# Reordering an expert loop: where a weights' copy, the first rows' turn and the optional pairs stand

## The reference

```python
# x: [2048, 256], E = 8 experts, top 2 of each token; w1, w3: [8, 256, 1024], w2: [8, 1024, 256]
logits = x @ gate_w
mult, sel = _sparse_mixer_routing(logits)
w = jnp.sum(mult[:, :, None] * (sel[:, :, None] == jnp.arange(E)[None, None, :]), axis=1)
h = jax.nn.silu(jnp.einsum('th,ehf->etf', x, w1)) * jnp.einsum('th,ehf->etf', x, w3)
out = jnp.einsum('etf,efh,te->th', h, w2, w)
x = _layernorm(x + out)
```

## Time and profile before

| | us |
|---|---|
| median of 3 executions (700.98 to 705.46) | 701.7 |
| the profiled execution, its time | 703.86 |
| its span, first to last instruction | 701.9 |
| PE busy | 593.3 (85% of the span) |
| DVE busy | 452.1 (64%) |
| POOL busy | 282.4 (40%) |
| ACT busy | 245.5 (35%) |
| mean granted PE clock | 0.913 |

### The profile page before, as it was taken

How to read it: one execution, slowest core, us unless ns; L and a number is a source line. 1 busy time by engine, 2 the same in 40 slices (tenths; PEclk the granted TensorE clock), 3 DMA queues, 4 the chain that set the end, 5 groups by cost and what they waited for, 6 DMA issues and landing times.

```text
span 701.9 us, 14082 instructions
## 1 busy us (share of the span) xinstructions
PE 593.3 (85%) x3500; PEld 462.3 (66%) x3501; DVE 452.1 (64%) x1284; ACT 245.5 (35%) x471; POOL 282.4 (40%) x199
## 2 busy tenths in 40 slices
PE   6999899797798885376997989989899898999740
PEld 2444469485475664365876878878788787888640
DVE  2566688765748869865556747667577575767524
ACT  3555530012767542222223232332422324222204
POOL 7000020012444456574715666166661665721112
PEclk9999999899799786567998999999999999999965
DMA  8999409004000043221583948649496385455326
GB/s 271 326 335 336 126 1 241 0 1 180 2 1 1 31 174 128 99 99 47 125 229 68 257 73 218 148 82 256 70 260 117 61 233 126 90 97 92 52 32 223
DMA packets 80214, 93.17 MB, mean 133 GB/s; under 512 B 20912, under 2 KB 76080, under 8 KB 78128
## 3 DMA queue, kind: packets, MB, share of 16 engines
q1 hardware_dynamic: 63088, 78.80, 38.6%
q0 software_dynamic: 6864, 9.11, 7.4%
q10 hardware_dynamic: 10224, 4.79, 4.4%
HBM read 42.67 MB, written 31.67 MB: 106 GB/s over the span
## 4 chain that ended last, share of the span: by engine, by line
PE 60%; DVE 15%; issue 8%; ACT 5%; DMA 5%; ACTq 4%; POOL 2%; SPq 0%; DVEq 0%; POOLq 0%
PE bank L2288 23%; PE bank L2310 11%; PE bank L1869 7%; PE bank L2028 4%; DVE region L1334 2%; DVE region L1332 1%; ACTq L1133 1%; DMA xcol<-xcol 1%; PE bank L1919 1%; PE bank L1878 1%; DMA total<-region,rid 1%; PE bank L2177 1%; DVE small L1351 1%; PE bank L1885 1%; PE bank L2300 1%
## 5 line engine op out<-in xcount | busy, mean ns | idle before, releaser
L2288 PE MATMUL bank<-experts_w,experts_x 128*128 (+1 forms) x864 | 222.2, 408 | 18.6 <-DVE experts_x L1713 18.5
L2288 PEld LDWEIGHTS bank<-experts_w,experts_x 128*128 128x128 f32 x864 | 162.1, 194 | 54.5 <-issue 19.0
L888 POOL DMA_INDIRECT total<-region,rid x36 | 55.7, 1548 | 145.3 <-DVE region L1803 91.4
L2310 PEld LDWEIGHTS bank<-experts_w 128*128 128x128 f32 x840 | 107.2, 195 | 7.4 <-issue 4.5
L1779 DVE TENSOR_TENSOR xcol<-region,bank 128x512 f32<-128x512 f32 x72 | 49.4, 686 | 97.2 <-ACT region L1148 96.3
L2310 PE MATMUL bank<-experts_w 128*128 x840 | 108.6, 286 | 4.0 <-issue 4.0
L1148 ACT ACTIVATE region<-bank 128x512 f32<-128x512 f32 x72 | 42.2, 597 | 142.5 <-PE bank L2288 60.3
L761 POOL TENSOR_TENSOR small<-small 128x4 f32<-128x4 f32 (+5 forms) x19 | 25.0, 1318 | 108.0 <-DVE small L1343 87.5
L1154 ACT CAST experts_w<-bank 128x512 fp32r<-128x512 f32 x70 | 40.6, 586 | 68.2 <-DVE bank L1788 61.7
L1869 PE MATMUL bank<-xcol,region 128*128 128x512 f32 x128 | 57.9, 610 | 7.6 <-DMA xcol<-in_xT 6.0
L868 POOL TENSOR_TENSOR experts_w<-wstage,experts_w 128x4096 f32 x6 | 53.9, 8988 | 24.9 <-ACT experts_w L1163 24.9
(11 more groups left out here) (355 smaller groups left out, 897.3 us busy)
## 6 DMA issues: line engine op xcount, KB each, us to landing
xcol<-xcol SPq DMA_DIRECT2D x140, 128.0 KB
slots<-padrow SPq DMA_DIRECT2D x8, 2210.0 KB, 19.4
wstage<-in_w_exp SPq DMA_DIRECT2D x6, 2048.0 KB, 9.1
wstage<-in_w_exp SPq DMA_DIRECT2D x2, 3072.0 KB, 11.8
wstage<-in_w_exp SPq DMA_DIRECT2D x6, 1024.0 KB, 5.6
region<-slots ACTq DMA_DIRECT2D x36, 128.0 KB
xcol<-in_xT SPq DMA_DIRECT2D x4, 512.0 KB, 7.2
xtok<-in_x SPq DMA_DIRECT2D x1, 2048.0 KB, 13.6
```

The costliest lines, as they stand in the source:

```text
L888: pool.indirect_dma_start(out=total, out_offset=bass.IndirectOffsetOnAxis(ap=rid[:, s:s + 1], axis=0), in_=yout[:, s], in_offset=None, com ...
L2288: mm = pe.matmul(bank[2 * u + m][:, :], (xTh, xTl)[a][:, s, k, :], moving(off, w, m * KD * F + k * F + u * HALF, HALF), start=(k == 0 and ...
L2310: mm = pe.matmul(bank[6][:, 0:D], (high, low)[a][:, u, c, :], moving(off, w, 2 * KD * F + (4 * u + c) * D, D), start=(u == 0 and c == 0 an ...
```

## The change

- **ACT:** a block opens with `silu(g, 0)`; then the row load, `silu(g, 1)`, `high_turned(g-1)`, and `high_up(g)` at the end.
- **Rows:** one transfer of 260 columns into `xg` takes the place of the two; it waits for both the turned rows and the metadata of the block whose buffer it takes. DVE works out `row_meta(g+1)` in block g and keeps the result in `kept` (`keep_meta`). `rows(g+1)` stands ahead of `middle(g, 0)`.
- **Weights:** 2048 + 2048 + 2048 columns are loaded in blocks g+1, g+2, g+3 behind an event block g, each after its own part is used up; `tab_load` becomes a mask of three bits. POOL's order is `send_block(g-2)`, `split_down(g-1)`, `low_up(g)`, the last in two halves.
- **Start:** PE turns block 0's rows ahead of the early down; `row_meta(0)` moves ahead of the loop.
- **Loops:** `all_pairs` runs the optional pairs first and the 14 required ones behind them, with the number of optional ones in a register `more`.

```diff
+        def all_pairs(eng, pair):
+            more = eng.value_load(tab_n[0:1, 3:4], min_val=0, max_val=NB // 2 - SURE)
+            with eng.Fori(0, NB // 2 - SURE) as it:
+                with eng.If(more - it > 0):
+                    pair(it + 2)
+            with eng.Fori(0, SURE - 2) as it:
+                pair(it + (more + 2))
...
             def load_ahead(g):
-                with sp.If(sp.value_load(tab_load[0:1, bass.ds(g - 1, 1)], min_val=0, max_val=1) > 0):
-                    event = event_of(g - 1)
-                    e = expert_of(event + 2)
-                    sp.wait_ge(w_low_up, event)
-                    load_up(e)
...
+                begun = sp.value_load(tab_load[0:1, bass.ds(g, 1)], min_val=0, max_val=7)
+                far = not isinstance(g, int) or g > 3
+                with sp.If(begun > 0):
+                    for n in range(2 if far else 1):
+                        with sp.If((begun & (1 << n)) > 0):
+                            event = event_of(g - (n + 1))
+                            e = expert_of(event + 2)
+                            sp.wait_ge(w_low_up, 2 * event + n)
+                            load_up(e, n)
+                    if far:
+                        with sp.If((begun & 4) > 0):
+                            event = event_of(g - 3)
+                            e = expert_of(event + 2)
+                            sp.wait_ge(w_ready, event + 2)
+                            load_down(e)
...
-                pool.tensor_tensor(lo_of(off)[:, 0:ACT_PART], wstage[:, 0:ACT_PART], hi_of(off).bitcast(F32)[:, 0:ACT_PART],
-                                   ALU.subtract).then_inc(w_low_up, 1)
+                for half in range(2):
+                    part = slice(half * UP_PART, (half + 1) * UP_PART)
+                    pool.tensor_tensor(lo_of(off)[:, part], wstage[:, part], hi_of(off).bitcast(F32)[:, part],
+                                       ALU.subtract).then_inc(w_low_up, 1)
...
+                    if not isinstance(g, int) or g >= 2:
+                        send_block(g - 2, s)
+                        with pool.If(begins(g - 1)):
+                            split_down(g - 1)
                     with pool.If(begins(g)):
                         low_up(g)
...
             def load_rows(g, s):
-                rows = slots[bass.ds(slot_of(g), P), :]
+                slot = slot_of(g)
                 act.wait_ge(xg_turned, g - 1)
-                act.dma_start(xq[:, s], rows[:, 0:D]).then_inc(xq_loaded[s], 16)
...
+                act.sem_inc(act_gate, 1)
+                act.wait_ge(meta_done, g - 1)
+                act.dma_start(xg[:, s], slots[bass.ds(slot, P), :]).then_inc(xg_loaded[s], 16)
...
                 for s in range(2):
                     g = 2 * p + s
-                    start = isinstance(g, int) and g < 2
-                    if start and g == 0:
-                        silu(g, 0)
+                    silu(g, 0)
+                    if isinstance(g, int) and g == 0:
                         silu(g, 1)
...
                     load_rows(g + 2, s)
-                    load_meta(g, s)
-                    if not start:
-                        high_up(g)
-                    silu(g, 0)
                     silu(g, 1)
                     for u in range(2):
                         high_turned(g - 1, u)
-                    if start:
-                        high_up(g)
+                    high_up(g)
...
-            dve.tensor_copy(tab_load[:, :], evblk[:, :])
+            link(dve.memset(cmps[:, 0:NB + 3, 0], 0.0))
+            for n in range(3):
+                link(dve.scalar_tensor_tensor(cmps[:, n + 1:n + 1 + NB, 0], evblk[:, :], float(1 << n), cmps[:, n + 1:n + 1 + NB, 0],
+                                              ALU.mult, ALU.add))
+            dve.tensor_copy(tab_load[:, :], cmps[:, 0:NB + 3, 0])
...
-                    row_meta(g - 1, 1 - s)
+                    rows(g + 1, 1 - s)
                     middle(g, s, 0)
-                    rows(g + 1, 1 - s)
+                    keep_meta(g - 1, 1 - s)
+                    row_meta(g + 1, 1 - s)
                     middle(g, s, 1)
...
                     mm = pe.transpose(o[:, c * P:(c + 1) * P], fmid[:, u, c * P:(c + 1) * P], ident[:, :])
                 fill(("fhT", u), mm)
+            turn_rows(0, 0)
             o = claim("fy")
...
                     if isinstance(g, int) and g == 0:
-                        turn_rows(g, s)
                         up(g, s, 0, slot_at[0])
...
-            with pe.Fori(0, SURE - 2) as it:
-                pair(it + 2)
-            with pe.Fori(0, NB // 2 - SURE) as it:
-                with pe.If(npair - it > SURE):
-                    pair(it + SURE)
+            all_pairs(pe, pair)
```

More of the change, by code:

```diff
@@ L450, in decoder_kernel @@
         w_up_loaded, w_down_loaded, w_low_up = (sem(n) for n in ("w_up_loaded", "w_down_loaded", "w_low_up"))
-        xq_loaded = [sem(f"xq{s}_loaded") for s in range(2)]
-        xm_loaded = [sem(f"xm{s}_loaded") for s in range(2)]
+        xg_loaded = [sem(f"xg{s}_loaded") for s in range(2)]
+        meta_kept = sem("meta_kept")
         grouped = [sem(f"h{s}_grouped") for s in range(2)]
@@ L598, in _ @@
                 sp.wait_ge(w_ready, 2)
-                load_up(expert_of(2))
+                e = expert_of(2)
+                for half in range(2):
+                    load_up(e, half)
             regroup(2, 0)
@@ L609, in pair @@
                 load_ahead(2 * p)
-            with sp.Fori(0, SURE - 2) as it:
-                pair(it + 2)
-            with sp.Fori(0, NB // 2 - SURE) as it:
-                with sp.If(npair - it > SURE):
-                    pair(it + SURE)
+            all_pairs(sp, pair)
             for s in range(2):
-                for landed, count in ((xq_loaded[s], 16 * npair + 16), (xm_loaded[s], 16 * npair), (y_sent[s], 16 * npair + 16 * s)):
+                for landed, count in ((xg_loaded[s], 16 * npair + 16), (y_sent[s], 16 * npair + 16 * s)):
                     sp.wait_ge(landed, count)
@@ L867, in low_up @@
                 pool.sem_inc(pool_gate, 1)
-                pool.tensor_tensor(lo_of(off)[:, 0:ACT_PART], wstage[:, 0:ACT_PART], hi_of(off).bitcast(F32)[:, 0:ACT_PART],
-                                   ALU.subtract).then_inc(w_low_up, 1)
+                for half in range(2):
+                    part = slice(half * UP_PART, (half + 1) * UP_PART)
+                    pool.tensor_tensor(lo_of(off)[:, part], wstage[:, part], hi_of(off).bitcast(F32)[:, part],
+                                       ALU.subtract).then_inc(w_low_up, 1)
             def split_down(g):
                 event, off = event_of(g), next_off(g)
-                pool.wait_ge(w_low_up, event)
+                pool.wait_ge(w_low_up, 2 * event + 1)
                 pool.wait_ge(w_down_loaded, 16 * event)
@@ L1775, in _, with keep_meta @@
             first_weigh()
+            row_meta(0, 0)
+            def keep_meta(g, s):
+                dve.wait_ge(meta_done, g + 1)
+                if not isinstance(g, int) or g >= 2:
+                    dve.wait_ge(yout_done, g - 1)
+                dve.tensor_copy(kept[:, s], meta[:, s, 3:5]).then_inc(meta_kept, 1)
             def middle(g, s, u):
@@ L2246, in first_up, with turn_rows @@
                     fill((name, u), mm)
+            def turn_rows(g, s):
+                pe.wait_ge(xg_loaded[s], 8 * (g - s) + 16)
+                if isinstance(g, int) and g == 0:
+                    wait_drained(pe, ("f3", 1))
+                else:
+                    pe.wait_ge(xgT_done, g)
+                for k in range(KD):
+                    mm = pe.transpose(bank[7][:, k * P:(k + 1) * P], xg[:, s, k * P:(k + 1) * P], ident[:, :])
+                mm.then_inc(xg_turned, 1)
             turn_norm2(B - 2)
@@ L2291, in up @@
                 mm.then_inc(up_done, 1)
-            def turn_rows(g, s):
-                pe.wait_ge(xq_loaded[s], 8 * (g - s) + 16)
-                if isinstance(g, int) and g == 0:
-                    wait_drained(pe, ("f3", 1))
-                else:
-                    pe.wait_ge(xgT_done, g)
-                for k in range(KD):
-                    mm = pe.transpose(bank[7][:, k * P:(k + 1) * P], xq[:, s, k * P:(k + 1) * P], ident[:, :])
-                mm.then_inc(xg_turned, 1)
             def down(g, u, off, high, low):
```

96 lines of the change are left out of this document (32 added, 64 removed).

## The result

Over 20 executions of each kernel the changed one takes 701.8 us in the median and the one before 704.6; the ratio is 0.9957, with a 95% interval of 0.9938 to 0.9976. That is faster by 0.4%, about 3 us, and within 1%. The forecast was 3.9% faster (674.6, range 669 to 686): it was wrong.

What follows compares the result with a forecast made beforehand. PE alone was taken to bound ordinary blocks (8.68 us), with stalls where experts begin. Terms -24.3 + 1.6 - 4.5 - 4.5 + 4.6 = -27.1 us took the profiled 703.86 to 676.8, or 674.6 against the median; range 669 to 686.

Steps and rivals of the forecast that it cites:

- Silus open, copy ends: six events: ACT at the six blocks beginning an expert: copying weights after the Silus removes PE's stalls and slow matmuls, -24.3 us.
- ready weights late behind four-block experts: POOL's chain of low parts readies weights 0.8 us late after four-block experts; two of three pay, +1.6 us.
- start of the expert stage: Turning first rows ahead of the early down brings tables and block 1's rows sooner: -4.5 us (bounds 0 and -6).
- skip in the middle: Skipping six optional pairs between blocks 7 and 8 idles PE 3.3 us, plus 1.3 slow matmuls: +4.6 us.
- skip gone from the end: Without skipped pairs behind the loop, DVE's last product starts 4.0 us sooner, final matmuls run faster: -4.5 us.
- The slack of 1.0 us: Block after a weights' copy: the late Silu's product frees PE's bank at G+16.3; PE wants it at G+17.4.
- The lead: PE's sequencer reaches the loop's end 2.3 us before the last matmul ends, so only that much skipping hides.
- Rival 1: The optional-pair skip hides in PE's instruction queue, so the +4.6 vanishes: 670.0 us, chance 0.10.
- the late Silu (2): Silu behind the weights' copy comes late anyway, stalling each expert 1 to 2 us: 684 to 688, chance 0.09.
- the ready weights (3): Ready weights bound short experts; three stall 2 to 3 us, +6 to +9: 681 to 684, chance 0.10.
- the ordinary period is 8.68 us (5): Slower: extra registers for block numbers eat PE's sequencer lead, lengthening 28 blocks; 1.5 us each gives 717, chance 0.03.
- The early turn (4): Turning first rows early brings nothing, because landing scatters, not tables, hold block 1's row load: 679 us, chance 0.06.

Runs made afterwards that it cites:

- K: The changed kernel with the metadata kept by two one-column tensor_scalar instructions instead of one two-column tensor_copy, same place and waits: 682.3 us, 0.9658 of before.

## Why the prediction was wrong, step by step

| step | forecast, us | K's profile, us |
|---|---|---|
| Silus open, copy ends: six events | -24.3 | -24.4 |
| ready weights late behind four-block experts | +1.6 | +1.2 |
| start of the expert stage | -4.5 | -2.4 |
| skip in the middle | +4.6 | +6.0 |
| skip gone from the end | -4.5 | -4.7 |
| sum | -27.1 | -24.3 |
| the kept copy | 0 | not in K; +22.9 in the changed kernel |

- **The step that failed** is in the first part: "DVE's copy of the metadata is one short instruction on an engine that waits for ACT in each block. I price these ... at nothing." Its own 0.16 us is short indeed; its wait for POOL is not in the sum. From block 3's turned rows to those turned in the last block the changed kernel takes 319.0 us and K 296.1: 22.9 us. The copy's excess in the changed kernel is 52.2 - 36 x 0.16 = 46 us on DVE, half of which reaches PE. One of my signs of being wrong came true, the gaps at the copies reappearing one block later (1.53 us at 381.97), but for this reason and not for a late Silu. I had no rival for it, and none of the six cases with a time held the result: I gave "same" 0.03.
- **The events** came out as worked out. In the kernel before the six event periods exceed 8.68 by 24.4 us, in K by nothing but the +1.2 and the loss at block 4 that the table counts under the start. The slack of 1.0 us held: K's waits for a product sum to 0.5 us. That ACT's order is worth 9.5 us in K and costs 6% alone in the kernel before shows that several edits share this gain, and that they lean on one another; the sum was right, the working went by ACT's order and the rows' place alone.
- **Ready weights:** 9.27 and 9.26 us instead of 8.68 behind two of the four-block experts, 0.6 each (forecast 0.8), the third covered by the skip. Right: with the optional pairs last that third one waits 0.93 us.
- **Start:** from the early down to block 2's turned rows K is 4.8 us faster (16.0 us against 20.8), the 4.3 that I had and a little more. Around block 4 it loses 2.4, where I had a part of 0.9. The mis-sized term is that loss, and the early turn is not what brings it: with the first rows turned late it is 4.7 us. It falls from 2.6 to 0.9 us when block 2's regrouping goes ahead of the loads of expert 2, so by these two profiles the order in SP's queue is most of it. Why the kernel before, with that regrouping behind the same loads, shows no such loss on PE stays open.
- **Optional pairs first:** PE idles 4.20 us in the middle, not 3.3, and resumes at 4.60 us for 12 matmuls: 14.69 - 8.68 = 6.0. The lead was as forecast. K's sequencer reached the skip loop at 393.2, 2.3 us before the last matmul ended at 395.5, and left it 4.5 us later, at 397.7. What I had too small is what stands behind it: 2.0 us to the first up at 399.72, where I had 1.1. Rival 1, that the skip hides in PE's queue, fell: the gap is there in every kernel with this order. The move as a whole loses about 3 us, where I had it at +0.1.
- **The other rivals** fell too. In K the late Silu (2) costs at most those 0.5 us, the ready weights (3) wait 0.3 us each, and the ordinary period is 8.68 us (5). The early turn (4) is worth 5.8 us by the middle values.
- **Sum:** K stands at 0.9658, 24 us below before, against my 27.1. Its 682 us lies inside the range of 669 to 686 given for the change, but that kernel was not the one forecast.

## What to carry to other kernels

Beside each instruction that is added on DVE, look at what POOL runs at that moment, not only at its duration: two columns of metadata waited up to 8.8 us for low parts of weights. Keep such values one column at a time, or place them where POOL is idle. And an order on one engine is not a change by itself: moving the weights' copy to the end of ACT's block cost 6% where POOL's consumer of it still stood ahead of the sending, and gained in K, where it stands behind.

## What the runs showed of the hardware

- A DVE instruction over two float32 columns in SBUF, with one input or two, lasted until POOL's `tensor_tensor` ended, and through a whole row of them where they overlapped (8.80 us, about seven); over one column it took 0.15 us in the same place of DVE's order. The second product, with an input in the PSUM bank, ran beside POOL's second half in 0.69 us (381.03).
- PE's sequencer was 2.3 us ahead of the matmuls when it came to the skip of the optional pairs, in the middle (393.2 and 395.5) as at the end. With 4.5 us for the skip and 2.0 us behind it, 4.2 us of idle time remained.
